# Graph and expert network on one core: the modulation moved one turn later on VectorE, and rows loaded four tiles ahead in the last row stage

## The chip, the core and the metric

The kernel is one program for one core of a Trainium2 chip. Its time is the device time of one execution in microseconds (us). Of the kernel before there are three runs: 3177.03 us in the median, 3170.88 the lowest, 3182.74 the highest. One more execution was recorded by the profiler, and all rows below are from it. The engines named here are PE (TensorE, matrix products and transposes), DVE (VectorE), ACT (ScalarE), POOL (GpSimd) and SP (SyncE, which here only issues transfers).

## What is computed

The reference adds four layers to `x` (1250 rows of 512 numbers): a graph layer over 20000 edges, a spline layer that sends each row to one of 64 experts, a graph transformer of four blocks, and a feed-forward layer with ternary weights. The change touches only the graph transformer's work on rows:

```python
def _cond_layer_norm(x, cond, sw, sb, bw, bb):
    mu = jnp.mean(x, axis=-1, keepdims=True)
    var = jnp.var(x, axis=-1, keepdims=True)
    xn = (x - mu) * jax.lax.rsqrt(var + EPS)
    return xn * (1.0 + (cond @ sw + sb)) + (cond @ bw + bb)

for i in range(4):
    y = _cond_layer_norm(x, cond, s1_w[i], s1_b[i], b1_w[i], b1_b[i])
    x = x + _sparse_attention(y, src, dst, wq[i], bq[i], wk[i], bk[i], wv[i], bv[i], wo[i], bo[i])
    y = _cond_layer_norm(x, cond, s2_w[i], s2_b[i], b2_w[i], b2_b[i])
    x = x + (jax.nn.relu(y @ m_w1[i] + m_b1[i]) @ m_w2[i] + m_b2[i])
```

The transformer's input is itself the normalised `x`, and `x` is added to its result at the end.

## The kernel before, in words

The 1250 rows are ten tiles of 125. Rows that don't fit on the chip's buffers lie in two tensors in device memory: `g_d` holds the transformer's running rows, `x_d` the rows of the layer around it. Between the attentions, which this change leaves alone, stands one function, `rows_stage`. It runs nine times:

- **the first stage** ("first" to "qkv"), once: the rows lie in a buffer already; norm, modulation, then the projections to queries, keys and values.
- **the attn-to-mlp stages**, four times: output projection of the attention added to the rows, norm, modulation, first half of the MLP.
- **the mlp-to-qkv stages**, three times: second half of the MLP added to the rows, norm, modulation, projections for the next block.
- **the last stage** ("mlp" to "final"), once: second half of the MLP, the rows of `g_d` and those of `x_d` summed and stored in `x_d`. It has no norm.

In a stage each engine has a written list of turns, one for each tile t from 0 to 9. Semaphores alone order the engines against each other; each engine does its own list strictly in order. With norm, the work on a tile goes through these steps (names of the code):

- SP `load(t)`: the tile's rows from `g_d` into one of four slots `g_row`. POOL adds a bias row (L1598).
- PE `src(t)`: the product that is added to the rows (L1470); not in the first stage.
- DVE `add(t)`: adds the product (L1806), then `bn_stats` and `bn_aggr` (L1808, L1810). SP then stores the rows to `g_d` (L1568).
- ACT `deviation(t)`, DVE `scales(t)` (L1814, L1816), ACT `center(t)` (L1708): the normalised row, in one of four slots `y_row`.
- PE `cond(t)`: 1+scale and bias of the condition, two products into two banks (L1632). There is one pair of banks, so `cond(t)` waits until `modulate(t-1)` has read it.
- DVE `modulate(t)`: y times scale plus bias, two instructions (L1823, L1825).
- PE `turn(t)`: four transposes of the row tile (L690). ACT `high(t)` copies them rounded (L1713), DVE `low(t)` takes the rest (L1829).
- PE `unit(n)`: twelve products of the turned rows with a weight matrix (L1461), from turn 7 on one for each turn, and after the turns all that are left. In the mlp stages ACT `take(n)` and DVE `finish(n)` (L1837) split each result.

In turns 3 to 6 DVE also splits a slice of the weights (`split`, L1797 or L1799).

The slots `g_row` are four. SP's list in the stages with norm, after the first four loads, is for each tile: wait for `added`, store tile t, then `load(t + 4)`, which first waits until that very store has landed, since the slot is the same. SP stands still in that wait, and the store of tile t+1 is behind it. In the last stage the list before is: store tile t, then `load(t + 2)`, whose slot was stored two turns earlier, and a load of the tile's `x_d` rows into one of two slots.

Of the kernel before, what the change touches and what calls it, by code (L numbers as in the profile page):

```python
# [18 lines left out]
ALU = mybir.AluOpType  # L19
# [3 lines left out]
P = 125  # L23
NT = N // P
# [1490 lines left out]
def rows_stage(nc, T, M, source, sink, g_d, x_d, loads, late, bias, bqk, bvo):  # L1515
# [5 lines left out]
    NCH = len(PARTS)  # L1521
    three = sink == "qkv"
    names = ("cw_in cw_ready cw_next b_in a_in w_in v_in a_high a_cut b_high b_cut v_high v_cut k_high k_cut "
             "g_in0 g_in1 g_in2 g_in3 gst0 gst1 gst2 gst3 x_in0 x_in1 o_high o_cut biased made added "
             "step std_s scale_s centered scaled row turned copied lowered "
             "unit_made taken h_high h_cut v_made v_row v_top v_low spare")
    with Stage(nc, names) as (cw_in, cw_ready, cw_next, b_in, a_in, w_in, v_in, a_high, a_cut, b_high, b_cut, v_high, v_cut,
                              k_high, k_cut, g_in0, g_in1, g_in2, g_in3, gst0, gst1, gst2, gst3, x_in0, x_in1,
                              o_high, o_cut, biased, made, added, step, std_s, scale_s, centered, scaled, row, turned,
                              copied, lowered, unit_made, taken, h_high, h_cut, v_made, v_row, v_top, v_low, spare):  # L1530
        g_in, gst, x_in = (g_in0, g_in1, g_in2, g_in3), (gst0, gst1, gst2, gst3), (x_in0, x_in1)
        cols = lambda t: slice(t * P, (t + 1) * P)
        turn_bank = lambda t: T.ps[:, 4 + t % 2, 0:4 * P].rearrange("p (c n) -> p c n", c=4)
        norm = sink != "final"
# [1 line left out]
        g = (lambda t: M.g[:, t % 4, :]) if pe_source else (lambda t: M.first[:, t, :])  # L1536
# [7 lines left out]
        with nc.Block() as block:  # L1544
            @block.sync
            def _(sp):
                def load(t):
                    if t >= 4:
                        if norm:
                            sp.wait_ge(centered, t - 3)  # L1550
                        sp.wait_ge(gst[t % 4], 16 * (t // 4))
                    sp.dma_start(g(t), g_d[t * P:(t + 1) * P, :]).then_inc(g_in[t % 4], 16)
                    if sink == "final":
                        if t >= 2:
                            sp.wait_ge(biased, t - 1)
                        sp.dma_start(M.y[:, t % 2, :], x_d[t * P:(t + 1) * P, :]).then_inc(x_in[t % 2], 16)
                ahead = 2 if sink == "final" else 4
                if pe_source:
                    load(0)
                    load(1)  # L1560
                if norm:
                    loads(sp, cw_in, b_in, w_in)
                if pe_source:
                    for t in range(2, ahead):
                        load(t)
                    for t in range(NT):
                        sp.wait_ge(added, t + 1)
                        sp.dma_start((g_d if norm else x_d)[t * P:(t + 1) * P, :], g(t)).then_inc(gst[t % 4], 16)  # L1568
                        if t + ahead < NT:
                            load(t + ahead)  # L1570
                if norm:
                    late(sp, cw_ready, cw_next, made, a_in, unit_made, v_in)
                if pe_source:
                    for t in range(NT - 4, NT):
                        sp.wait_ge(gst[t % 4], 16 * (t // 4 + 1))
                else:
                    sp.wait_ge(T.spilled, 64)

            @block.gpsimd
            def _(pool):  # L1580
                def o_lo(t):
                    pool.wait_ge(o_high, t + 1)
                    if t >= 3:
                        pool.wait_ge(made, t - 2)
                    nc.gpsimd.tensor_tensor(M.o[1][:, t % 3, :, :], M.q[:, :, cols(t)], M.o[0][:, t % 3, :, :].bitcast(F32),
                                            ALU.subtract).then_inc(o_cut, 1)
                if pe_source:
                    if source == "attn":
                        o_lo(0)
                    for t in range(NT):  # L1590
                        if source == "attn" and t + 1 < NT:
                            o_lo(t + 1)
                        pool.wait_ge(g_in[t % 4], 16 * (t // 4 + 1))
                        if sink == "final":
                            pool.wait_ge(x_in[t % 2], 16 * (t // 2 + 1))
                            nc.gpsimd.tensor_tensor(g(t), g(t), M.y[:, t % 2, :], ALU.add).then_inc(spare, 1)
                            pool.wait_ge(spare, t + 1)
                        nc.gpsimd.tensor_tensor(g(t), g(t), bias, ALU.add).then_inc(biased, 1)  # L1598

# [183 lines left out]
            def _(dve):  # L1783
# [9 lines left out]
                def split(raw, parts, hi_sem, sem, scale=1.0, ks=range(KD)):  # L1793
                    for k in ks:
                        dve.wait_ge(hi_sem, k + 1)
                        if scale == 1.0:
                            v.tensor_tensor(parts[1][:, k, :], raw[:, k, :], parts[0][:, k, :].bitcast(F32), ALU.subtract).then_inc(sem, 1)  # L1797
                        else:
                            v.scalar_tensor_tensor(parts[1][:, k, :], raw[:, k, :], scale, parts[0][:, k, :].bitcast(F32),  # L1799
                                                   ALU.mult, ALU.subtract).then_inc(sem, 1)  # L1800

                def add(t):
                    if pe_source:
                        dve.wait_ge(biased, t + 1)
                        dve.wait_ge(made, t + 1)
                        v.tensor_tensor(g(t), T.ps[0:P, t % 2, :], g(t), ALU.add).then_inc(added, 1)  # L1806
                        dve.wait_ge(added, t + 1)
                    v.bn_stats(T.stats[:, t, :], g(t)).then_inc(step, 1)  # L1808
                    dve.wait_ge(step, 2 * t + 1)
                    v.bn_aggr(T.mv[:, t, :], T.stats[:, t, :]).then_inc(step, 1)  # L1810

                def scales(t):
                    dve.wait_ge(std_s, t + 1)
                    v.reciprocal(T.rstd[:, t:t + 1], T.std[:, t:t + 1]).then_inc(scale_s, 1)  # L1814
                    dve.wait_ge(scale_s, 2 * t + 1)
                    v.scalar_tensor_tensor(T.shift[:, t:t + 1], T.mv[:, t, 0:1], -1.0, T.rstd[:, t:t + 1],  # L1816
                                           ALU.mult, ALU.mult).then_inc(scale_s, 1)

                def modulate(t):
                    y = M.y[:, t % 4, :]  # L1820
                    dve.wait_ge(scaled, t + 1)
                    dve.wait_ge(centered, t + 1)
                    v.scalar_tensor_tensor(y, T.ps[0:P, 2, :], 1.0, y, ALU.add, ALU.mult).then_inc(spare, 1)  # L1823
                    dve.wait_ge(spare, t + 1)
                    v.tensor_tensor(y, y, T.ps[0:P, 3, :], ALU.add).then_inc(row, 1)  # L1825

                def low(t):
                    dve.wait_ge(copied, t + 1)
                    v.tensor_tensor(M.yp[1][:, :, cols(t)], turn_bank(t), M.yp[0][:, :, cols(t)].bitcast(F32),  # L1829
                                    ALU.subtract).then_inc(lowered, 1)  # L1830
# [13 lines left out]
                if source == "attn":  # L1844
# [2 lines left out]
                v.tensor_tensor(M.cwr[32:64, :, :], T.cw[32:64, :, :], M.cwr[32:64, :, :].bitcast(F32),  # L1847
                                ALU.subtract).then_inc(cw_ready, 1)
                for t in range(NT):
                    add(t)  # L1850
                    if t >= 1:
                        scales(t - 1)
                    if t >= 2:
                        modulate(t - 2)
                    if t >= 8:
                        finish(t - 8)
                    if t >= 3:
                        low(t - 3)
                    if 3 <= t < KD + 3:
                        split(M.raw_b, M.b, b_high, b_cut, -DH ** -0.5 if three else 1.0, [t - 3])  # L1860
                scales(NT - 1)
                modulate(NT - 2)
                finish(2)
                low(NT - 3)
                modulate(NT - 1)
                finish(3)
                low(NT - 2)
                finish(4)
                finish(5)
                low(NT - 1)  # L1870
# [234 lines left out]
def second_graph_net(nc, T, A, x_scope, pairs, mask_d, x_d, g_d):  # L2105

    with ExitStack() as ctx:
# [49 lines left out]
        def attend(L, last):  # L2157
# [4 lines left out]
            rows_stage(nc, T, M, "attn", "mlp", g_d, x_d, *mlp_loads(L, last), bvo[:, 1, :], bqk, bvo)  # L2162

        rows_stage(nc, T, M, "first", "qkv", g_d, x_d, *qkv_loads(0, True), None, bqk, bvo)
        with nc.Fori(0, 3) as L:
            attend(L, False)
# [354 lines left out]
```

## Time and profile before

| | us |
|---|---|
| median of 3 runs | 3177.03 (3170.88 to 3182.74) |
| profiled execution, its own time | 3176.09 |
| its span, first to last instruction | 3174.4 |
| PE busy in the span | 2592.4 (82%) |
| DVE busy | 1889.8 (60%) |
| ACT busy | 1357.3 (43%) |
| POOL busy | 1127.8 (36%) |
| hardware queue of the transfers, share of 16 engines | 21.1% |

The nine row stages lie between 1077 and 2872 us of the span, with the four attentions between them. Busy shares of the whole span are means over stages with different limits, so what follows is read stage by stage from rows in order of time. A row of such a view has the start in us, the duration in us, the engine, the line, the operation, what it writes and reads, the count, and in brackets how long the engine had been idle before it and which instruction ended that wait.

### The profile page before, as it was taken

How to read it: one execution, taken by the hardware profiler on the slowest of the kernel's cores; microseconds unless marked ns; L12 is line 12 of the kernel's file. 1: busy time of each engine (PE TensorE's matmuls, PEld its weight loads, DVE VectorE, ACT ScalarE, POOL GpSimd, SP SyncE). 2: the span in 40 equal slices, each digit the busy share in tenths (PEclk: the TensorE clock that was granted, in tenths of full speed). 3: DMA queues.
4: the chain of work that ended last, by engine and by line, in shares of the span. 5: the costliest groups of instructions: out<-in, count | busy, mean ns of one | idle time of the engine just before them, and what ended most of it. 6: DMA issues, size and time to landing. Idle time of an engine off the chain costs nothing. (4 is left out here: it accounts for less than half of the span.)

```text
span 3174.4 us, 39503 instructions
## 1 busy us (share of the span) xinstructions
PE 2592.4 (82%) x13585; PEld 2210.9 (70%) x13585; DVE 1889.8 (60%) x3557; ACT 1357.3 (43%) x2706; POOL 1127.8 (36%) x886
## 2 busy tenths in 40 slices
PE   3999998347564299988889978989888899864999
PEld 3777877247364287876778966878767788653997
DVE  2899997523823536765456765367654567615862
ACT  2566664301343235653346643356543466412431
POOL 2777775856833002231012231022310122322420
PEclk9999999668677599999999999999999999886999
DMA  7344442157287302012211032120122110223101
GB/s 244 81 85 77 85 79 56 8 151 214 31 246 228 111 17 80 17 47 87 75 50 32 17 95 73 40 81 17 43 89 77 49 33 17 95 82 88 51 21 33
DMA packets 183070, 246.11 MB, mean 78 GB/s; under 512 B 110269, under 2 KB 118904, under 8 KB 175443
## 3 DMA queue, kind: packets, MB, share of 16 engines
q1 hardware_dynamic: 91312, 196.19, 21.1%
q0 software_dynamic: 91552, 47.27, 7.3%
q8 instruction: 118, 1.93, 0.3%
q14 instruction: 88, 0.72, 0.1%
HBM read 189.90 MB, written 52.95 MB: 77 GB/s over the span
## 5 line engine op out<-in xcount | busy, mean ns | idle before, releaser
L2101 POOL TENSOR_SCALAR prob<-prob,rden,linked 125x1250 f32<-125x1250 f32 x160 | 223.6, 1397 | 938.2 <-DVE rden L2068 938.2
L579 POOL DMA_INDIRECT pairs<-late_cnt,late_idx x160 | 345.2, 2157 | 124.2 <-issue 68.5
L2019 ACT CAST prob_high<-ps 125x375 fp32r<-125x375 f32 (+1 forms) x480 | 230.9, 503 | 266.8 <-PE ps L1981 266.5
L2060 DVE CUSTOM_DVE_ANT_0 prob<-ps,mask 125x1250 f32<-125x1250 f32 x160 | 233.1, 1457 | 124.9 <-PE ps L1957 111.5
L2073 DVE TENSOR_TENSOR prob_low<-ps,prob_high 125x375 fp32r<-125x375 f32 (+1 forms) x480 | 269.6, 585 | 46.6 <-ACT prob_high L2019 46.6
L338 POOL DMA_INDIRECT Hg<-h_rows,dsti x160 | 226.1, 1413 | 132.1 <-issue 93.7
L1970 PE MATMUL ps<-ident,prob 125*125 125x125 f32 x1600 | 252.4, 273 | 17.3 <-POOL prob L2101 10.6
L538 PE MATMUL ps<-onehot,mhi 125*128 125x512 f32 (+1 forms) x960 | 246.3, 365 | 9.7 <-DVE onehot L426 9.2
L1970 PEld LDWEIGHTS ps<-ident,prob 125*125 125x125 f32 x1600 | 232.4, 187 | 29.8 <-POOL prob L2101 22.9
L538 PE MATMUL ps<-onehot,mlo 125*128 125x512 f32 (+1 forms) x960 | 239.4, 358 | 0.0
L2011 ACT ACTIVATE prob<-prob,top 125x1250 f32<-125x1250 f32 x160 | 214.7, 1342 | 41.1 <-DVE top L2060 32.1
L1598 POOL TENSOR_TENSOR g_row<-g_row,bvo 125x512 f32<-125x512 f32 x80 | 103.7, 1296 | 351.9 <-DMA g_row<-g_d 350.8
L1981 PE MATMUL ps<-prob_high,v_high 125*128 125x376 f32 (+1 forms) x480 | 211.0, 440 | 4.6 <-ACT qT L2023 3.0
L1632 PE MATMUL ps<-cwr,condT 81*125 81x512 f32 x160 | 62.0, 472 | 180.3 <-DVE y_row L1825 98.2
L1957 PE MATMUL ps<-k_high,q_high 128*125 128x512 f32 (+1 forms) x480 | 174.2, 363 | 29.5 <-DVE q_low L2049 25.2
L538 PEld LDWEIGHTS ps<-onehot,mhi 125*128 125x128 f32 x960 | 158.8, 191 | 47.1 <-issue 18.4
L538 PEld LDWEIGHTS ps<-onehot,mlo 125*128 125x128 f32 x960 | 157.8, 191 | 28.3
L1957 PE MATMUL ps<-k_low,q_high 128*125 128x512 f32 (+1 forms) x480 | 172.5, 359 | 0.0
L1957 PE MATMUL ps<-k_high,q_low 128*125 128x512 f32 (+1 forms) x480 | 171.9, 358 | 0.0
L1632 PEld LDWEIGHTS ps<-cwr,condT 81*125 81x125 f32 x160 | 28.2, 205 | 205.1 <-DVE y_row L1825 120.2
L1981 PE MATMUL ps<-prob_high,v_low 125*128 125x376 f32 (+1 forms) x480 | 169.0, 352 | 0.0
L1981 PE MATMUL ps<-prob_low,v_high 125*128 125x376 f32 (+1 forms) x480 | 169.0, 352 | 0.0
(409 smaller groups left out, 6140.3 us busy)
## 6 DMA issues: line engine op xcount, KB each, us to landing
mask<-mask_d SPq DMA_DIRECT2D x40, 546.9 KB
g_row<-g_d SPq DMA_DIRECT2D x80, 250.0 KB
g_d<-g_row SPq DMA_DIRECT2D x70, 250.0 KB
sg_wd<-L_ffn_Wd SPq DMA_DIRECT2D x32, 512.0 KB
w_ring<-L_ffn_Wd SPq DMA_DIRECT2D x16, 1024.0 KB
w_ring<-L_ffn_Wu SPq DMA_DIRECT2D x16, 1024.0 KB
pairs<-zeros POOLq DMA_DIRECT2D x18, 625.0 KB, 26.2
keyrow<-keys_d SPq DMA_DIRECT2D x40, 244.1 KB
```

The lines of the kernel that those rows point to most:

```text
L338: nc.gpsimd.indirect_dma_start(Hg[:, g % 2, j, :, :].rearrange("p c f -> p (c f)"), None, h_rows[:, :], bass.IndirectOffsetOnAxis(dsti[:, ...
L538: ins = nc.tensor.matmul(agg_chunk(T, a, c), part[:, u, j, a * 128:(a + 1) * 128], onehot[:, j, n0:n0 + nn], start=first and k == 0 and c < 2,
L579: nc.gpsimd.indirect_dma_start(pairs[a][:, :], bass.IndirectOffsetOnAxis(T.E.late_idx[:, c:c + 1], 0), T.E.late_cnt[:, c:c + 1], None, com ...
L1598: nc.gpsimd.tensor_tensor(g(t), g(t), bias, ALU.add).then_inc(biased, 1)
L1957: ins = nc.tensor.matmul(S(u)[0:P, n0:n0 + nn], M.qr[x][:, b % 2, i * P:(i + 1) * P], M.k[y][:, h, n0:n0 + nn], start=n == 0, stop=n == 2)
L1970: ins = nc.tensor.transpose(T.ps[0:P, 3 + s % 4, i * P:(i + 1) * P], M.prob[:, (FIRST[b] + i) % RING, j * P:(j + 1) * P], T.ident[0:P, 0:P])
L1981: ins = nc.tensor.matmul(T.ps[:, 7, 0:w], M.v[x][:, j, h * DH:(h + 1) * DH], M.pt[y][:, s % 3, 0:w], start=j == 0 and n == 0, stop=j == NT ...
L2011: s.activation(M.prob[:, u % RING, :], M.prob[:, u % RING, :], ACT.Exp, bias=M.top[:, u % RING:u % RING + 1], scale=-1.0, accum_out=M.den[ ...
L2019: s.copy(M.pt[0][:, n % 3, 0:w], T.ps[0:P, 3 + n % 4, 0:w]).then_inc(high, 1)
L2060: v.tensor_tensor_reduce(M.prob[:, r, :], S(u)[0:P, 0:N], M.mask[:, it % MASKS, :], 1.0, 3.0e38, ALU.add, ALU.min, M.top[:, r:r + 1]).then ...
L2073: v.tensor_tensor(M.pt[1][:, n % 3, 0:w], T.ps[0:P, 3 + n % 4, 0:w], M.pt[0][:, n % 3, 0:w].bitcast(F32), ALU.subtract).then_inc(low, 1)
L2101: nc.gpsimd.tensor_scalar(M.prob[:, r, :], M.prob[:, r, :], M.rden[:, r:r + 1], T.linked[:, it:it + 1], ALU.mult, ALU.mult).then_inc(norme ...
```

## The change

It has two parts. In the stages with norm DVE's `modulate` of a tile moves: turn t no longer has `modulate(t-2)` after `scales(t-1)`, but begins with `modulate(t-3)`, ahead of `add(t)`; the calls behind the loop move with it. In the last stage `x_d` rows get four slots and four semaphores instead of two, and both loads run four tiles ahead. The lists of PE, ACT and POOL are the same.

```diff
                     if sink == "final":
-                        if t >= 2:
-                            sp.wait_ge(biased, t - 1)
-                        sp.dma_start(M.y[:, t % 2, :], x_d[t * P:(t + 1) * P, :]).then_inc(x_in[t % 2], 16)
-                ahead = 2 if sink == "final" else 4
+                        if t >= 4:
+                            sp.wait_ge(biased, t - 3)
+                        sp.dma_start(M.y[:, t % 4, :], x_d[t * P:(t + 1) * P, :]).then_inc(x_in[t % 4], 16)
...
-                    for t in range(2, ahead):
+                    for t in range(2, 4):
                         load(t)
...
-                        if t + ahead < NT:
-                            load(t + ahead)
+                        if t + 4 < NT:
+                            load(t + 4)
...
                 for t in range(NT):
+                    if t >= 3:
+                        modulate(t - 3)
                     add(t)
                     if t >= 1:
                         scales(t - 1)
-                    if t >= 2:
-                        modulate(t - 2)
                     if t >= 8:
                         finish(t - 8)
                     if t >= 3:
                         low(t - 3)
                     if 3 <= t < KD + 3:
                         split(M.raw_b, M.b, b_high, b_cut, -DH ** -0.5 if three else 1.0, [t - 3])
+                modulate(NT - 3)
                 scales(NT - 1)
-                modulate(NT - 2)
                 finish(2)
                 low(NT - 3)
-                modulate(NT - 1)
+                modulate(NT - 2)
                 finish(3)
                 low(NT - 2)
+                modulate(NT - 1)
```

DVE in the first stage, one turn (3 to 6), before: the modulation stands between `shift` and `y_low`.

```order
 L1808 BN_STATS stats<-first_rows 125x6
 L1810 BN_AGGR mv<-stats 125x2
 L1814 RECIPROCAL rstd<-std 125x1
 L1816 SCALAR_TENSOR_TENSOR shift<-mv,rstd 125x1
 L1823 SCALAR_TENSOR_TENSOR y_row<-ps,y_row 125x512
 L1825 TENSOR_TENSOR y_row<-y_row,ps 125x512
 L1829 TENSOR_TENSOR y_low<-ps,y_high 128x4x125
 L1799 SCALAR_TENSOR_TENSOR set_b_low<-set_b_raw,set_b_high 128x512
```

The same turn now (the new file's lines are one lower):

```order
 L1822 SCALAR_TENSOR_TENSOR y_row<-ps,y_row 125x512
 L1824 TENSOR_TENSOR y_row<-y_row,ps 125x512
 L1807 BN_STATS stats<-first_rows 125x6
 L1809 BN_AGGR mv<-stats 125x2
 L1813 RECIPROCAL rstd<-std 125x1
 L1815 SCALAR_TENSOR_TENSOR shift<-mv,rstd 125x1
 L1828 TENSOR_TENSOR y_low<-ps,y_high 128x4x125
 L1798 SCALAR_TENSOR_TENSOR set_b_low<-set_b_raw,set_b_high 128x512
```

Before, the `y_low` of turn t was of the tile that had been modulated in turn t-1; now it is of the tile whose modulation opens the same turn.

DVE in an attn-to-mlp stage, turn 9 and what stands behind it, before:

```order
 L1806 TENSOR_TENSOR g_row<-ps,g_row 125x512
 L1808 BN_STATS stats<-g_row 125x6
 L1810 BN_AGGR mv<-stats 125x2
 L1814 RECIPROCAL rstd<-std 125x1
 L1816 SCALAR_TENSOR_TENSOR shift<-mv,rstd 125x1
 L1823 SCALAR_TENSOR_TENSOR y_row<-ps,y_row 125x512
 L1825 TENSOR_TENSOR y_row<-y_row,ps 125x512
 L1837 TENSOR_TENSOR inner_low<-inner_row,inner_high 128x500
 L1829 TENSOR_TENSOR y_low<-ps,y_high 128x4x125
```

And now, from the same `add`:

```order
 L1805 TENSOR_TENSOR g_row<-ps,g_row 125x512
 L1807 BN_STATS stats<-g_row 125x6
 L1809 BN_AGGR mv<-stats 125x2
 L1813 RECIPROCAL rstd<-std 125x1
 L1815 SCALAR_TENSOR_TENSOR shift<-mv,rstd 125x1
 L1836 TENSOR_TENSOR inner_low<-inner_row,inner_high 128x500
 L1828 TENSOR_TENSOR y_low<-ps,y_high 128x4x125
 L1822 SCALAR_TENSOR_TENSOR y_row<-ps,y_row 125x512
 L1824 TENSOR_TENSOR y_row<-y_row,ps 125x512
```

The modulation of tile 7 now stands behind `finish` and `low`. In the mlp-to-qkv stages `finish` has no instruction there, and it stands behind `low` alone.

SP in the last stage, its first rows before:

```order
 L1552 DMA g_row<-g_d 125x512
 L1556 DMA y_row<-x_d 125x512
 L1552 DMA g_row<-g_d 125x512
 L1556 DMA y_row<-x_d 125x512
 L1568 DMA x_d<-g_row 125x512
 L1552 DMA g_row<-g_d 125x512
 L1556 DMA y_row<-x_d 125x512
```

And now:

```order
 L1556 DMA y_row<-x_d 125x512
 L1552 DMA g_row<-g_d 125x512
 L1556 DMA y_row<-x_d 125x512
 L1552 DMA g_row<-g_d 125x512
 L1556 DMA y_row<-x_d 125x512
 L1567 DMA x_d<-g_row 125x512
 L1552 DMA g_row<-g_d 125x512
 L1556 DMA y_row<-x_d 125x512
```

Four pairs of loads stand ahead of the first store instead of two, and the pair behind a store is of the tile four further on.

## Rows read from the trace of the kernel before

**Rows 1.** First stage by window: busy us of PE, PEld, DVE, ACT, POOL; clock.

```profile
1079.00:1103.00 24.00, 14.91 (x43) 10.48 (x44) 22.57 (x56) 11.83 (x24) 0.00 (x0) 0.52 0.03 12
```

**Rows 2.** First stage in order of time: first modulation, then a turn from the third.

```profile
1082.44 0.69 DVE L1823 SCALAR_TENSOR_TENSOR y_row<-ps,y_row 125x512 f32<-125x512 f32 x1
...
1088.87 0.69 DVE L1823 SCALAR_TENSOR_TENSOR y_row<-ps,y_row 125x512 f32<-125x512 f32 x1
...
1089.59 0.69 DVE L1825 TENSOR_TENSOR y_row<-y_row,ps 125x512 f32<-125x512 f32 x1
...
1090.20 0.67 DVE L1829 TENSOR_TENSOR y_low<-ps,y_high 128x500 fp32r<-128x500 f32 x1
...
1090.34 1.22 PE L1632 MATMUL ps<-cwr,condT 81*125 81x512 f32 x2 [1.65 <-DVE y_row L1825]
1090.79 0.68 DVE L1799 SCALAR_TENSOR_TENSOR set_b_low<-set_b_raw,set_b_high 128x512 fp32r<-128x512 f32 x1
...
1091.35 1.04 PE L690 MATMUL ps<-ident,y_row 125*128 125x125 f32 x4
...
1092.42 0.58 ACT L1713 CAST y_high<-ps 128x500 fp32r<-128x500 f32 x1 [1.71 <-PE ps L690]
```

**Rows 3.** First stage in order of time, PE when the units begin.

```profile
1097.50 1.22 PE L1632 MATMUL ps<-cwr,condT 81*125 81x512 f32 x2 [1.53 <-DVE y_row L1825]
...
1103.30 0.63 PE L1632 MATMUL ps<-cwr,condT 81*125 81x512 f32 x2
...
1106.92 0.63 PE L1632 MATMUL ps<-cwr,condT 81*125 81x512 f32 x2
```

**Rows 4.** Second attn-to-mlp stage in order of time, behind the last tile's add.

```profile
1892.56 0.69 DVE L1806 TENSOR_TENSOR g_row<-ps,g_row 125x512 f32<-125x512 f32 x1 [3.04 <-POOL g_row L1598]
...
1895.08 0.69 DVE L1825 TENSOR_TENSOR y_row<-y_row,ps 125x512 f32<-125x512 f32 x1
1895.68 0.67 DVE L1837 TENSOR_TENSOR inner_low<-inner_row,inner_high 128x500 fp32r<-128x500 f32 x1
...
1895.83 0.73 PE L1632 MATMUL ps<-cwr,condT 81*125 81x512 f32 x2 [3.54 <-DVE y_row L1825]
...
1896.28 0.67 DVE L1829 TENSOR_TENSOR y_low<-ps,y_high 128x500 fp32r<-128x500 f32 x1
...
1901.11 0.63 PE L1632 MATMUL ps<-cwr,condT 81*125 81x512 f32 x2
```

**Rows 5.** First mlp-to-qkv stage in order of time, behind the last tile's add.

```profile
1546.50 1.22 PE L1632 MATMUL ps<-cwr,condT 81*125 81x512 f32 x2 [3.38 <-DVE y_row L1825]
```

**Rows 6.** First attn-to-mlp stage, SP's own issues in order of time.

```profile
1415.94 0.25 SPq L1552 DMA_DIRECT2D g_row<-g_d  x1
1416.23 0.34 SPq L1568 DMA_DIRECT2D g_d<-g_row  x1
1423.10 0.25 SPq L1552 DMA_DIRECT2D g_row<-g_d  x1
```

**Rows 7.** Same stage, SP's waits: total us, times, longest us.

```profile
SPq L1551 <- DMA g_d<-g_row: 41.5, 6, 7.8
```

**Rows 8.** Last stage from 2806 to 2866 us, bytes moved in 40 slices.

```profile
GB/s 36 45 63 126 124 130 128 126 128 117 67 71 117 126 130 128 126 128 109 75 46 105 127 128 127 128 128 127 105 45 93 126 128 128 126 128 130 108 104 38
```

**Rows 9.** Last stage in order of time: SP's issues, and POOL's first sums.

```profile
2796.38 0.27 SPq L1552 DMA_DIRECT2D g_row<-g_d  x1
...
2802.91 1.26 POOL L1596 TENSOR_TENSOR g_row<-g_row,y_row 125x512 f32<-125x512 f32 x1 [37.10 <-DMA y_row<-x_d]
...
2806.27 0.25 SPq L1568 DMA_DIRECT2D x_d<-g_row  x1
...
2860.66 6.26 SPq L1568 DMA_DIRECT2D x_d<-g_row  x2
...
2863.32 1.26 POOL L1596 TENSOR_TENSOR g_row<-g_row,y_row 125x512 f32<-125x512 f32 x1 [3.41 <-DMA y_row<-x_d]
...
2871.86 0.36 SPq L2220 DMA_DIRECT2D raw<-L_ffn_w_gate  x1
```

More of the change, by code:

```diff
@@ L1523, in rows_stage @@
     names = ("cw_in cw_ready cw_next b_in a_in w_in v_in a_high a_cut b_high b_cut v_high v_cut k_high k_cut "
-             "g_in0 g_in1 g_in2 g_in3 gst0 gst1 gst2 gst3 x_in0 x_in1 o_high o_cut biased made added "
+             "g_in0 g_in1 g_in2 g_in3 gst0 gst1 gst2 gst3 x_in0 x_in1 x_in2 x_in3 o_high o_cut biased made added "
              "step std_s scale_s centered scaled row turned copied lowered "
@@ L1527, in rows_stage @@
     with Stage(nc, names) as (cw_in, cw_ready, cw_next, b_in, a_in, w_in, v_in, a_high, a_cut, b_high, b_cut, v_high, v_cut,
-                              k_high, k_cut, g_in0, g_in1, g_in2, g_in3, gst0, gst1, gst2, gst3, x_in0, x_in1,
+                              k_high, k_cut, g_in0, g_in1, g_in2, g_in3, gst0, gst1, gst2, gst3, x_in0, x_in1, x_in2, x_in3,
                               o_high, o_cut, biased, made, added, step, std_s, scale_s, centered, scaled, row, turned,
                               copied, lowered, unit_made, taken, h_high, h_cut, v_made, v_row, v_top, v_low, spare):
-        g_in, gst, x_in = (g_in0, g_in1, g_in2, g_in3), (gst0, gst1, gst2, gst3), (x_in0, x_in1)
+        g_in, gst, x_in = (g_in0, g_in1, g_in2, g_in3), (gst0, gst1, gst2, gst3), (x_in0, x_in1, x_in2, x_in3)
         cols = lambda t: slice(t * P, (t + 1) * P)
@@ L1594, in _ @@
                         if sink == "final":
-                            pool.wait_ge(x_in[t % 2], 16 * (t // 2 + 1))
-                            nc.gpsimd.tensor_tensor(g(t), g(t), M.y[:, t % 2, :], ALU.add).then_inc(spare, 1)
+                            pool.wait_ge(x_in[t % 4], 16 * (t // 4 + 1))
+                            nc.gpsimd.tensor_tensor(g(t), g(t), M.y[:, t % 4, :], ALU.add).then_inc(spare, 1)
                             pool.wait_ge(spare, t + 1)
```

## The prediction

> **What bounds the kernel now.** I read the views in this order: the page's slices for where the row stages lie, then each kind of row stage in order of time, then SP's own issues and waits, because there the engines are idle together. I looked for the instruction that the next one waits for, at the places where the change cuts a list.
>
> The first stage is bound by DVE until the units begin: it is busy 22.57 of 24.00 us, while PE has 14.91 us of work at a granted clock of 0.52, which is mostly the lower level of 1.2 GHz [rows 1]. A turn there is a chain over three engines as well. DVE's two modulation instructions start at 1088.87 and 1089.59 and end at 1090.28; PE's `cond` starts at 1090.34, the transposes at 1091.35, and they end at 1092.39; ACT's copy runs from 1092.42 to 1093.00 [rows 2]. Before, nothing in the same turn needs that copy. From the first unit on PE is the bound: `cond` to `cond` is 1106.92 - 1103.30 = 3.62 us [rows 3].
>
> The seven other stages with norm are paced by SP. In the cycle load, store, wait for the store, next load, SP needs 1423.10 - 1415.94 = 7.16 us [rows 6], and it stands in that wait 41.5 us in six times, at most 7.8 each [rows 7]. DVE and PE idle in them, until the last tile's `add`. Behind that PE is the bound again: it has idled 3.54 us when `modulate(7)` lets `cond(8)` go at 1895.83 [rows 4], 3.38 us in the other kind of stage [rows 5]; from there it has units without a pause to the stage's end.
>
> The last stage is bound by transfers. In the full slices they move 126 to 130 GB/s and never more [rows 8]. One tile's 125 x 512 f32 are 256,000 bytes, so a transfer takes 2.0 us at 128 GB/s and a tile's three take 6.0. The thin slices (36 to 75 GB/s) are where the next three have not been issued soon enough.
>
> **Part 1, DVE's order, first stage.** Nothing is added or removed; two instructions move by one place. Now `low(t-3)` needs, in its own turn, what the opening modulation starts. From the start of `modulate`: 1.47 us to `cond`, 1.01 to the transposes, 1.04 for them, 0.03, 0.58 for the copy, 0.03: `low` can start 4.16 us after it. Then 0.59 to `split` (1090.79 - 1090.20) and as much to the next modulation: 5.34 us for a turn [rows 2]. The statistics and `scales`, some 1.1 us, are hidden in that. The first modulation starts at 1082.44 in either order, since nothing is between `scales(1)` and it. Before, the fifth starts at 1097.50 - 1.47 = 1096.03, 13.59 us later [rows 2, 3]. Now it is 4 x 5.34 = 21.36 us later. The difference, 7.8 us, is how much later `cond(5)`, and so the first unit, runs. From unit 0 the same loop runs at the high clock: 1.47, 0.46 + 0.59 for the products (half of 1.01 and the transposes alike), 0.6 for the copy, 0.59 for `low` is about 3.7 against PE's 3.62, so 0.1 for each of three turns. I take +8.1 us; bounds are 1.1 (only the two calls that now stand ahead of `modulate(4)`, `low` and `split`, if the loop doesn't bind) and 10.
>
> **Part 1, the seven stages paced by SP.** In turns 4 to 9 DVE now does the moved modulation at once after the former turn, in the 3 us for which it waits for POOL [rows 4], so `add` starts when it did, and SP's cycle is untouched. PE runs its `cond` later and has idle time for it. What is late is the last turn: `cond(8)` waits for `modulate(7)`, and ahead of this now stand `finish(1)` and `low(6)` in the attn-to-mlp stages, 0.60 us each (1895.68 to 1896.28, and as long for `low`) [rows 4], and `low(6)` alone in the mlp-to-qkv stages. PE has no other work there. 4 x 1.2 + 3 x 0.6 = +6.6 us. The next one, `modulate(8)` behind `low(7)`, ends about 5.2 us after `cond(8)` starts and `cond(9)` is due 5.28 us after it [rows 4], so it just fits. If it doesn't, each stage loses up to 1 us more; if PE's later start is made up elsewhere, nothing is lost. Bounds 0 and 14.
>
> **Part 2, the last stage.** Two more pairs of loads go out at the start. Then for each tile SP issues store t, waits until it has landed, and only then loads tile t+4. Before, the slot had been stored two turns earlier and that wait was over. The trace shows the new cycle in the other stages, with one load: 7.16 us, of which 4.0 are two transfers and 3.2 the time until the store counts as landed [rows 6]. With two loads I take 6.0 + 3.2 = 9.2 us, against (2863.32 - 2802.91) / 9 = 6.7 for a tile before [rows 9]. For a load the tail is 2802.91 - 2796.38 - 4.0 = 2.5 us [rows 9].
> - Store 0 is the ninth transfer from 2796.38 (eight loads are ahead of it; it is issued at 2806.27) [rows 9]: landed at 2796.4 + 18.0 + 3.2 = 2817.6.
> - Load of tile 4 at 2817.6, of tile 9 five cycles later, at 2863.6; its `x_d` rows landed at 2863.6 + 4.0 + 2.5 = 2870.1.
> - From there to the next stage's first issue it is 2871.86 - 2863.32 = 8.5 us now [rows 9]. To it come 0.8 us, since stores 6, 7 and 8 are then queued behind the last loads, where before it was one: 2879.4 against 2871.86, +7.5 us.
>
> Tiles 2 and 3 get their rows sooner, and the last ones later. The bounds: -11.7 us, if SP never waits and 30 transfers run at 2.0 us from 2796.4 to 2856.4, plus 3.2 and the 0.6 to the next stage; +15, with the longest wait in every cycle (7.8 of wait and 0.6 of issues with one load [rows 7], 10.4 with two).
>
> The Trainium skill has a rule against my tail: "DMA: Bandwidth & Descriptors", section "Anatomy of one DMA", gives a DMA a fixed cost of about 2.0 us, most of it the receipt of the write, plus bytes by 436 GB/s. The row differs in both: 3.2 us behind the last byte, and 2.0 us for 256,000 bytes where the page's rate gives 0.6. By its 2.0 us alone the last stage would end as before, and the sum would be 3192 (an estimate from that page); by the rows it is 3199.
>
> **Sum.** 8.1 + 6.6 + 7.5 = 22.2 us. Against the profiled execution's own 3176.1 us (span 3174.4) that is 3198.3; that execution lies 0.9 under the median of the three runs, so I predict **3199 us**.
>
> **Rivals.**
> - *B, SP's wait costs nothing and the queue stays full.* Place: the last stage; -11.7 us there, decided if the loads of tiles 4 to 9 go out before the queue runs dry. Then 14.7 - 11.7 leaves 3180: not slower. For it: 12 us of the stage are thin slices [rows 8]. Against: SP stands in just this wait in seven stages [rows 7].
> - *C, a store lands as soon as a load does.* A tail of 2.5 instead of 3.2 in six cycles takes 4.2 us off: 3195. For it: only one shape of cycle is shown. The skill's rule named above stands here, with 3192.
> - *D, PE's pauses cost clock as well.* `cond(8)` to `cond(9)` is 5.28 us where it could be 3.62 at the high level [rows 3, 4]; all of it at 1.2 GHz would be 7.2. Then seven stages lose 2 us more: 3213. Against: PE's idle time before `cond(8)` stays as long as it was, since `cond(7)` is later too.
> - *E, faster.* B in the last stage, and the moved modulation finds PE's products done and gives back the waits inside the turns: nothing lost in the norm stages and a few us won, 3160. For it: DVE has `cond` one turn longer to wait for. Against: DVE is busy 94% of the first stage [rows 1] and waits for POOL in the others [rows 4].
>
> **How the numbers follow.** Forecast 0.62, B 0.12, C 0.14, D 0.08, E 0.04. The forecast's own range is 3190 to 3209: its three terms by their nearer bounds, and 3 us of spread between runs. With B partly left out and C and D taken in, the range is 3184 to 3209. What a measurement can tell from no change is 0.5%, 3161.1 to 3192.9. Slower than that: all but a tenth of the forecast, D, and part of C, less what I allow for errors common to all: 0.66. Within: B, the rest of C and of the forecast: 0.30. Faster: 0.04.
>
> **What would show it.** In the first stage modulations 5.3 us apart instead of 3.6, DVE idle before `y_low` with ACT's copy as releaser, and the first unit near 1107. In the attn-to-mlp stages `add` 7 to 8 us apart as now, and `cond(8)` 4.5 us behind the start of the last `add` instead of 3.27 (1895.83 - 1892.56) [rows 4]; in the mlp-to-qkv stages 3.9. In the last stage four pairs of loads, then SP issues 9.2 us apart, released by the store to `x_d`. I am wrong if those issues are under 7 us apart, if the units of the first stage start within 2 us of now, or if `add` in the seven stages moves.

## The result and the profile after

The changed kernel takes 3193.66 us in the median of its runs (3189.76 to 3203.71), the kernel before 3175.15 us beside it. The ratio is 1.0067, 95% interval 1.0056 to 1.0078, which is 21 us (it leaves out one disturbed run of the kernel before, which the median holds); the medians themselves lie 18.5 us apart. The forecast was 3199 us, with 0.66 on slower.

| profiled execution | before | after |
|---|---|---|
| own time, us | 3176.09 | 3193.53 |
| span | 3174.4 | 3191.8 |
| span before the first row stage | 1077.2 | 1072.8 |
| last row stage, first issue to the next stage's | 75.5 | 81.4 |

The two spans differ by 17.4 us, but the part ahead of the first row stage, which the change leaves alone, ran 4.4 us shorter in the execution after. So everything from the first row stage on took 21.8 us more, near what the ratio says. Lines of the new file are one lower than those of before.

**First stage.** One row by window, which answers to [rows 1] (busy us of PE, of PEld, which is PE's loading of weights, and of DVE, ACT and POOL; then the granted clock, the busy share of the 16 DMA engines, and GB/s):

```profile
1078.00:1102.00 24.00, 9.27 (x27) 6.21 (x28) 16.65 (x39) 8.94 (x18) 0.00 (x0) 0.50 0.02 8
```

DVE has 16.65 us of work in 24 where it had 22.57. The same stretch in order of time (start, duration, engine, line, operation; in brackets the idle time before and what ended it), for [rows 2]:

```profile
1088.76 0.68 DVE L1822 SCALAR_TENSOR_TENSOR y_row<-ps,y_row 125x512 f32<-125x512 f32 x1
1089.48 0.69 DVE L1824 TENSOR_TENSOR y_row<-y_row,ps 125x512 f32<-125x512 f32 x1
...
1090.22 1.22 PE L1631 MATMUL ps<-cwr,condT 81*125 81x512 f32 x2 [3.30 <-DVE y_row L1824]
...
1091.24 1.03 PE L690 MATMUL ps<-ident,y_row 125*128 125x125 f32 x4
1092.31 0.58 ACT L1712 CAST y_high<-ps 128x500 fp32r<-128x500 f32 x1 [3.36 <-PE ps L690]
...
1092.92 0.68 DVE L1828 TENSOR_TENSOR y_low<-ps,y_high 128x500 fp32r<-128x500 f32 x1 [1.69 <-ACT y_high L1712]
...
1093.52 0.68 DVE L1798 SCALAR_TENSOR_TENSOR set_b_low<-set_b_raw,set_b_high 128x512 fp32r<-128x512 f32 x1
...
1094.12 0.68 DVE L1822 SCALAR_TENSOR_TENSOR y_row<-ps,y_row 125x512 f32<-125x512 f32 x1
```

The loop can be walked with a finger: modulation, `cond`, transposes, ACT's copy, `y_low`, `split`, and the next modulation 5.36 us after the last. `y_low` waits 1.69 us, released by ACT's copy, and PE's wait before `cond` has grown to 3.30 us. PE when the units begin, for [rows 3]:

```profile
1100.93 1.21 PE L1631 MATMUL ps<-cwr,condT 81*125 81x512 f32 x2 [3.30 <-DVE y_row L1824]
...
1106.87 0.64 PE L1631 MATMUL ps<-cwr,condT 81*125 81x512 f32 x2
...
1110.63 0.73 PE L1631 MATMUL ps<-cwr,condT 81*125 81x512 f32 x2
...
1118.68 0.73 PE L1631 MATMUL ps<-cwr,condT 81*125 81x512 f32 x2 [0.28 <-DVE y_row L1824]
```

`cond(5)`, the first of these rows, stands 22.88 us behind the first modulation (1078.05), where it stood 15.06 behind (1097.50 - 1082.44): +7.8 us. From `cond(6)` at 1106.87 to `cond(9)` at 1118.68 it takes 11.81 us, where it took 10.89 before, and the last row shows PE waiting there for the late modulation. From the first modulation to the attention's first product the stage takes 118.82 us against 109.84, +9.0.

**Seven stages paced by SP.** The second attn-to-mlp stage behind its last `add`, for [rows 4], and under it the row of the first mlp-to-qkv stage, for [rows 5]:

```profile
1898.80 0.69 DVE L1805 TENSOR_TENSOR g_row<-ps,g_row 125x512 f32<-125x512 f32 x1 [3.28 <-POOL g_row L1597]
...
1900.60 0.67 DVE L1836 TENSOR_TENSOR inner_low<-inner_row,inner_high 128x500 fp32r<-128x500 f32 x1
1901.18 0.67 DVE L1828 TENSOR_TENSOR y_low<-ps,y_high 128x500 fp32r<-128x500 f32 x1
1901.77 0.68 DVE L1822 SCALAR_TENSOR_TENSOR y_row<-ps,y_row 125x512 f32<-125x512 f32 x1
1902.49 0.69 DVE L1824 TENSOR_TENSOR y_row<-y_row,ps 125x512 f32<-125x512 f32 x1
...
1903.23 0.72 PE L1631 MATMUL ps<-cwr,condT 81*125 81x512 f32 x2 [3.76 <-DVE y_row L1824]
...
1908.51 0.63 PE L1631 MATMUL ps<-cwr,condT 81*125 81x512 f32 x2
```

```profile
1552.37 0.78 PE L1631 MATMUL ps<-cwr,condT 81*125 81x512 f32 x2 [3.17 <-DVE y_row L1824]
```

`finish` and `low` now stand ahead of `modulate(7)`, and `cond(8)` starts 1903.23 - 1898.80 = 4.43 us behind the last `add` instead of 3.27; in the other kind of stage it is 1552.37 - 1548.54 = 3.83 us instead of 3.27. `cond(9)` follows 5.28 us later, as before. SP's issues (marked SPq) and its wait in the first attn-to-mlp stage, for [rows 6, 7]:

```profile
1420.93 0.25 SPq L1552 DMA_DIRECT2D g_row<-g_d  x1
1421.22 0.34 SPq L1567 DMA_DIRECT2D g_d<-g_row  x1
1428.32 0.25 SPq L1552 DMA_DIRECT2D g_row<-g_d  x1
```

```profile
SPq L1551 <- DMA g_d<-g_row: 41.0, 6, 7.8
```

Nothing moved there: 41.0 us of wait against 41.5.

**Last stage.** Bytes moved in 40 slices of 1.5 us from 2817 us on (for [rows 8]), then SP's waits in it (total us, times, longest):

```profile
GB/s 127 127 126 126 124 124 108 12 57 127 96 113 107 11 76 120 79 111 113 8 56 128 105 111 105 10 66 127 109 126 75 14 85 126 108 126 55 26 109 116
```

```profile
SPq L1552 <- DMA x_d<-g_row: 49.3, 6, 10.3
```

Once in every six slices the transfers fall to 8 to 26 GB/s. In most of such a slice nothing is queued: SP waits for the store that it has just sent. In order of time, for [rows 9]:

```profile
2807.45 0.27 SPq L1552 DMA_DIRECT2D g_row<-g_d  x1
...
2813.34 1.80 SPq L1556 DMA_DIRECT2D y_row<-x_d  x1
...
2813.85 1.26 POOL L1595 TENSOR_TENSOR g_row<-g_row,y_row 125x512 f32<-125x512 f32 x1 [37.12 <-DMA y_row<-x_d]
...
2817.20 0.38 SPq L1567 DMA_DIRECT2D x_d<-g_row  x1
...
2827.89 0.25 SPq L1552 DMA_DIRECT2D g_row<-g_d  x1
2828.18 0.34 SPq L1556 DMA_DIRECT2D y_row<-x_d  x1
2828.57 0.34 SPq L1567 DMA_DIRECT2D x_d<-g_row  x1
2836.80 0.25 SPq L1552 DMA_DIRECT2D g_row<-g_d  x1
...
2872.10 0.25 SPq L1552 DMA_DIRECT2D g_row<-g_d  x1
...
2879.25 1.26 POOL L1595 TENSOR_TENSOR g_row<-g_row,y_row 125x512 f32<-125x512 f32 x1 [6.45 <-DMA y_row<-x_d]
...
2888.80 0.36 SPq L2220 DMA_DIRECT2D raw<-L_ffn_w_gate  x1
```

The first store is in and the next load goes out 20.4 us after the stage's first issue; then five cycles of (2872.10 - 2827.89) / 5 = 8.84 us.

### The profile page after: what moved, and what is told of

It is laid out like the page before. It is cut to its first block and busy times, and to the rows that moved or that the text cites. A ratio compares the mean times of both kernels' runs of the same rounds, so it can differ in the third digit from the quotient of the medians.

```text
span 3191.8 us, 39507 instructions
## 1 busy us (share of the span) xinstructions
PE 2594.4 (81%) x13585; PEld 2213.3 (69%) x13585; DVE 1885.8 (59%) x3557; ACT 1357.8 (43%) x2706; POOL 1144.3 (36%) x886
## 5 line engine op out<-in xcount | busy, mean ns | idle before, releaser
L579 POOL DMA_INDIRECT pairs<-late_cnt,late_idx x160 | 353.9, 2212 | 120.7 <-issue 69.4
```

Source lines behind the costliest of these rows:

```text
L579: nc.gpsimd.indirect_dma_start(pairs[a][:, :], bass.IndirectOffsetOnAxis(T.E.late_idx[:, c:c + 1], 0), T.E.late_cnt[:, c:c + 1], None, com ...
```

## The experiments

Ratios are to the kernel before on the same chip, with 95% intervals. Each theory's words stand as they were written ahead of the run.

**Each part alone.** `late_mod` puts the change's moves on DVE under a condition. The first of the two lines is that of the run with the first stage alone, the second that of the run with the seven; the other moves are put under `late_mod` in the same way.

```diff
+                late_mod = source == "first"
...
+                late_mod = source != "first"
...
+                    if late_mod and t >= 3:
+                        modulate(t - 3)
```

> Only the first stage has the new order on VectorE, everything else is as before. My account (the modulation opens a loop modulate, cond, transposes, ACT's copy, low, split of 5.34 us that DVE can't leave): cond(5) 22.9 us behind the first modulation instead of 15.1, and the whole kernel +7.8 us, 0.25%. Rival, that the order only shifts two calls and the loop doesn't bind: +1 us. Rival, that the difference lies outside the row stages (code loading, another start): under 2 us and no change of that distance.

Measured: 3184.39 against 3173.02 us, ratio 1.003 (1.0017 to 1.0043). From the first modulation, 1079.02, to `cond(5)`, 1101.90, it is the same 22.88 us as in the whole change, and to the attention's first product 118.48 us.

> Only the seven later stages with norm have the new order on VectorE, the first and the last are as before. My account: add times as before, cond(8) 4.43 us behind the last add in the four attn-to-mlp stages and 3.84 in the three mlp-to-qkv stages instead of 3.27; in sum 4 x 1.16 + 3 x 0.57 = +6.4 us, 0.2%. Rival, that DVE's later modulation holds the adds up: adds further apart than 7.3 us and more than +12. Rival, that PE makes it up: 0.

Measured: 3180.55 us, ratio 1.0026 (1.0012 to 1.0039). `cond(8)` stands 4.43 us behind the last `add` in all four attn-to-mlp stages and 3.84 in the three others: 4 x 1.16 + 3 x 0.58 = 6.4 us. The `add`s didn't move: first to last they take 370.6 us in the seven stages together, against 372.7 before.

> Only the last stage is changed: loads four tiles ahead, four slots for the x_d rows. My account (SP stands in the wait for the store that it has just issued): issues of g_row loads 8.8 us apart from tile 4 on, +6 us, 0.19%. Rival, that more transfers in flight run each slower: the full slices under 126 GB/s. Sum of this run and the two beside it should be the whole change, +20 us.

The edit is the change's part 2 alone. Measured: 3180.59 us, ratio 1.0019 (1.0006 to 1.0033). Issues to load tiles 4 to 9 go out from 2816.98 to 2862.01, 9.0 us apart, and the stage takes 82.8 us against 75.5, +7.4 where the whole change had +5.9. The three parts sum to +0.75%, the whole is +0.67%, each with some 0.12 of doubt: within that they add up.

**Is it the loop, in the first stage?** If `low` of a tile goes one turn later as well, the loop is open again while the modulation stays late.

```diff
-                    if t >= 3:
-                        low(t - 3)
+                    if t >= 3 + late_mod:
+                        low(t - 3 - late_mod)
```

> The first stage has the late modulation as in the run with the first stage alone, but low also stands one turn later (low(t-4) in turn t), so that no call of a turn needs what the opening modulation of the same turn starts. My account (the loop over three engines costs, not the modulation's place): modulations 3.58 us apart again, cond(5) 15.2 us behind the first modulation, the whole kernel 0 to +1 us against before. Rival, that beginning the turn with the modulation costs by itself (it delays statistics and scales, and with them center): still +5 us or more.

Measured: 3177.73 against 3177.55 us, ratio 1.0 (0.9991 to 1.001). The last modulation ahead of the units, and its `cond(5)`, in order of time:

```profile
1098.28 0.69 DVE L1823 SCALAR_TENSOR_TENSOR y_row<-ps,y_row 125x512 f32<-125x512 f32 x1
...
1099.74 1.22 PE L1632 MATMUL ps<-cwr,condT 81*125 81x512 f32 x2 [1.52 <-DVE y_row L1825]
```

It is 15.17 us behind the first modulation (1084.57), against 15.06 before, and the second to the fifth modulation stand 3.57 us apart. The late modulation by itself costs nothing, within 0.1%; what costs is that the same turn needs what ACT makes of its result.

**Is it only the two calls, in the seven stages?** Turns 3 to 8 have the late modulation. Turn 9 has both, `modulate(6)` at its head and `modulate(7)` at its old place, and the calls behind the loop are as before.

```diff
-                    if t >= 2:
+                    if (not late_mod and t >= 2) or (late_mod and t == NT - 1):
                         modulate(t - 2)
```

> The seven later stages with norm have the late modulation, but turn 9 also has modulate(7) directly behind scales(8), and the calls behind the loop are as before; first and last stage as before. My account (only the calls ahead of modulate(7) cost): cond(8) 3.27 us behind the last add in all seven, the whole kernel 0 against before. Rival, that the late modulation of turns 4 to 8 pushes PE back and the tail inherits it: cond(8) later than 3.27, still +3 us or more.

Measured: 3175.05 us, ratio 0.9994 (0.9985 to 1.0002). `cond(8)` in the second attn-to-mlp stage, whose last `add` starts at 1880.32:

```profile
1883.59 0.72 PE L1632 MATMUL ps<-cwr,condT 81*125 81x512 f32 x2 [2.36 <-DVE y_row L1825]
```

It is 3.27 us again, and the whole kernel's time is that of before. The late modulation in the turns is free there; only what stands ahead of `modulate(7)` is paid. In two of the seven stages `cond(9)` also follows 1.6 us sooner than before, 3.1 us in sum that the account doesn't name; the places of `cond(8)` are the firmer proof.

**The store that SP waits for.** With four slots, loads three tiles ahead need the slot of the tile before the one just stored.

```diff
-                ahead = 4 if sink == "final" else 4
+                ahead = 3 if sink == "final" else 4
```

> As the run with the last stage changed alone, but three tiles ahead instead of four. With three the slot was stored one turn earlier: when SP waits for that store, the transfers of one more tile are still queued behind it. My account: the queue never runs dry, issues 6.1 us apart, the last stage 9 us shorter than before and 15 shorter than with four: -9 us against before, 3167. Rival, that the depth itself costs (contention, more transfers in flight): between two and four ahead, so +3 us.

Measured: 3164.54 against 3173.02 us, ratio 0.9969 (0.9957 to 0.9981). Bytes moved in 40 slices of the last stage from 2796 us on, and SP's loads for two tiles:

```profile
GB/s 96 137 127 128 127 126 126 122 123 130 130 126 127 130 126 127 130 130 123 130 130 123 130 130 126 127 130 128 124 130 130 123 130 130 124 128 128 127 127 48
```

```profile
2810.91 0.25 SPq L1552 DMA_DIRECT2D g_row<-g_d  x1
...
2816.92 0.25 SPq L1552 DMA_DIRECT2D g_row<-g_d  x1
```

No thin slice is left, and a tile takes 6.0 us, three transfers of 2.0. The stage takes 65.2 us (2794.48 to 2859.70) against 75.5 before: -10.3 us, where rival B's price for a queue that stays full was -11.7. That one number, three instead of four, turns +0.19% into -0.31%: what the stage lost was lost in the empty queue.

**The 128 GB/s themselves.** The kernel has a helper, `wide` (L140), that sends a tile of 125 rows as two transfers, of 112 and of 13. Here it carries the last stage's transfers, the semaphores counting 32 for each tile; the loads are three tiles ahead.

```diff
+                def move(dst, src, sem):
+                    if WIDE:
+                        wide(sp, dst, src, sem)
...
-                    sp.dma_start(g(t), g_d[t * P:(t + 1) * P, :]).then_inc(g_in[t % 4], 16)
+                    move(g(t), g_d[t * P:(t + 1) * P, :], g_in[t % 4])
```

> Last stage alone, three tiles ahead, and each transfer of 125 rows issued as one of 112 rows and one of 13. My account (a transfer of 125 rows runs at 5 of the 16 engines' rate, 2.0 us, and that is what bounds the stage): full slices well over 130 GB/s, tiles 3 to 3.5 us apart, bound by POOL's two sums and PE, the stage 30 to 36 us shorter than before. Rival, that 128 GB/s is what rows of 2 KB get in any split: the same 6 us for a tile, and -9 us as with three ahead alone.

Measured: 3139.49 against 3177.55 us, ratio 0.9877 (0.986 to 0.9895). The same stretch of the stage, six tiles, by window in this kernel; the last two numbers are the busy share of the 16 DMA engines and GB/s:

```profile
2807.65:2825.10 17.45, 17.35 (x75) 13.23 (x74) 4.15 (x6) 0.00 (x0) 15.05 (x12) 1.00 0.85 252
```

and in the kernel with unsplit transfers and the same distance, five tiles:

```profile
2810.91:2840.96 30.05, 19.75 (x69) 13.95 (x67) 3.46 (x5) 0.00 (x0) 12.71 (x11) 0.89 0.33 128
```

Bytes flow at 252 instead of 128 GB/s, the DMA engines are busy 85% instead of 33% of the time, and the `add`s come 2.95 us apart ((2832.70 - 2806.14) / 9). PE is busy 17.35 of 17.45 us, at a granted clock of 1.00, the high level, and POOL 15.05: PE bounds the stage now. From its first issue to the next stage's it takes 38.15 us (2798.88 to 2837.03), 37.3 less than before, where 30 to 36 were expected.

> The order of before, the last stage three ahead, and every tile transfer of the eight stages in two pieces of 112 and 13 rows. My account: SP's cycle falls from 7.3 to about 5.2 us (3.2 of wait, 1.3 of transfers, the issues), and PE with 6.4 us for a turn takes over from turn 7 on: 8 to 11 us less in each of seven stages and 30 to 36 in the last, in sum -90 to -110 us, 3080. Rival, that the wait for the store hardly shrinks with the transfer: under 3 us in each of the seven.

The same for all transfers of tiles in the eight stages; DVE's order is as before, and the last stage's loads are three tiles ahead. Measured: 3035.26 against 3177.55 us, ratio 0.955 (0.9537 to 0.9564): 142 us less, the best of all kernels here. SP's wait in the first attn-to-mlp stage ([rows 7] before), and the last `add` with `cond(8)` and `cond(9)` there (lines are 8 higher):

```profile
SPq L1559 <- DMA g_d<-g_row: 11.9, 6, 2.3
```

```profile
1441.00 0.69 DVE L1814 TENSOR_TENSOR g_row<-ps,g_row 125x512 f32<-125x512 f32 x1 [2.05 <-PE ps L1470]
...
1444.36 0.63 PE L1640 MATMUL ps<-cwr,condT 81*125 81x512 f32 x2
...
1447.99 0.62 PE L1640 MATMUL ps<-cwr,condT 81*125 81x512 f32 x2
```

The wait for a store falls from 41.5 to 11.9 us, and what ends DVE's wait for `add` is now PE, not POOL. First to last `add` takes 40.7 us instead of 53.2 in this stage, and `cond(8)` to `cond(9)` 3.63 instead of 5.29. By window (the number behind the five engines is the granted clock), that stretch in the second attn-to-mlp stage before:

```profile
1895.83:1901.11 5.28, 5.28 (x18) 4.31 (x19) 3.91 (x8) 2.46 (x4) 0.00 (x0) 0.68 0.64 236
```

and the one above in this kernel:

```profile
1444.36:1447.99 3.63, 3.63 (x19) 3.03 (x19) 2.80 (x7) 2.27 (x4) 0.00 (x0) 1.00 0.80 247
```

PE had been idle 3.54 us before the first of these two windows [rows 4], and then works at a clock of 0.68, partly at 1.2 GHz; here, with no pause ahead of `cond(8)`, it works at 2.4 GHz. I had expected 90 to 110 us. Between the profiled spans there are 132: 86 by `add` spacing in seven stages (11.2 to 13.3 each, where 8 to 11 were expected), 13 by the stretch from the last `add` to `cond(9)` in them, which I had not counted, and 35 by the last stage (30.99 us from its first `add` to its end, before 66.31), against 2 the other way elsewhere.

**The change once transfers are fast.** Last, the whole change over the split transfers, and the split transfers with only the distance of four.

> The changed order in all stages with norm and the last stage four tiles ahead, with every tile transfer of the eight stages split 112+13. Against the kernel that has only the split transfers and three tiles ahead (its span 3042.4 us, ratio 0.955): first stage +7.8 us as before. In the seven others the calls ahead of modulate(7) still cost 4 x 1.2 + 3 x 0.6 = 6.6 us; and cond(9) is now due 3.63 us behind cond(8) where modulate(8) takes about 5.2, so up to 1.6 us more in each of seven, 11 us. Last stage: SP's wait for the store in each cycle, the difference that the kernel sent beside this one measures, about +10. Sum +35 us, span near 3078, ratio near 0.966. Rival: with SP no longer pacing (adds 5.5 us apart), DVE's order matters inside the turns, and having each cond one turn longer gives waits back: add spacing under 5.3 us, ratio 0.955 or less.

> Split transfers in all eight stages, the order of before, the last stage four tiles ahead instead of three: that one number is the difference from the kernel with ratio 0.955. Account of the dry queue: SP stands behind each store until it has landed; in the other stages with split transfers load to load is 3.9 us with one load, so with two about 5.2, against 3.0 a tile with three ahead. Six such cycles, less what the first loads gain: +10 us (8 to 14), ratio near 0.958. Rival: with fast transfers four pairs in flight cover the wait and nothing is lost: within 2 us of 0.955.

Measured against 3176.81 us: with the distance of four 3046.78 us, ratio 0.9598 (0.9575 to 0.9621); with the moved modulation as well 3068.8 us, ratio 0.9655 (0.9635 to 0.9675). The moved modulation costs 18 us here by the ratios, 22 by the medians, where 25 was expected. Of this the traces have 7.8 in the first stage up to `cond(5)`, 5.7 ahead of `cond(8)` in the seven (4 x 1.07 + 3 x 0.47), and a new wait: `cond(9)` comes 4.95 and 4.18 us behind `cond(8)` instead of 3.63, since `modulate(8)` is late, 4 x 1.32 + 3 x 0.55 = 6.9 us of the 11 allowed for. The first of the two products of `cond(9)` in the first attn-to-mlp stage, with the wait:

```profile
1451.78 0.50 PE L1640 MATMUL ps<-cwr,condT 81*125 81x512 f32 x1 [1.06 <-DVE y_row L1833]
```

In sum these are 20.4 us. The eight stages with norm are 25.3 longer in all; of the 4.9 us more, 3.8 are `add` spacing. First to last `add` takes 40.5 us in the attn-to-mlp stages, where it is 40.7 with the order of before (42.3 once), and 42.2 to 44.1 in the mlp-to-qkv stages, where it is 40.2 to 42.4. So the rival, waits given back inside the turns, finds at most 0.2 us in a stage and loses more elsewhere. The distance of four has load issues 2724.24 - 2700.53 = 23.7 us for five tiles, 4.74 each, where three ahead gives (2723.53 - 2706.00) / 6 = 2.92, and 38.78 us from the stage's first `add` to its end where it was 30.99: +7.8 us in the trace. By the ratios it is 0.48%, 15 us, with intervals 0.11% apart: a loss is shown, its size only roughly.

## Why the prediction was right

**First stage, +8.1 predicted.** The loop was worked out at 5.34 us from rows of before that never showed it closed, and it is 5.36; the later start of `cond(5)` was put at 7.8 and is 7.8. The run with `low` one turn later shows that the cause is this loop and not the order as such. The lesser claim, 0.1 for each of the three turns with units at the high clock, was too small: from `cond(6)` to `cond(9)` the steps are 3.77, 3.87 and 4.18 us in all three traces with the new order in this stage (within 0.02), and 3.62, 3.63 and 3.64 before, 0.9 more in sum instead of 0.3. The last step has `cond(9)` waiting for `modulate(8)`, which the sum had not counted here. So the term is 8.6 (the run with the first stage alone) to 9.0 us rather than 8.1.

**Seven stages, +6.6 predicted.** 6.4 by the traces of both the change and the run with this part alone: 0.58 us for each call instead of 0.60. The claims that hold it up held too: SP's wait is unchanged, `modulate(8)` just fits (it ends at 1908.12, `cond(9)` starts at 1908.51), and with the old order behind the last turn the loss is gone.

**Last stage, +7.5 predicted, 5.9 measured** (81.35 against 75.48 us). The mechanism was right and its size off by 1.6 in this trace; in that of the run with the last stage alone the stage has +7.4. The term that was off is the store's tail, the time from a store's last byte until SP goes on, 3.2 us, taken from a cycle with one load. With two loads the cycle is 8.84 us, a tail of 2.8, and behind the eight first loads it is 20.4 - 18.0 = 2.4. This brought the last load 2.5 us earlier than forecast (64.65 us behind the first issue, not 67.2). Against it, tile 9's rows took 7.15 us to land where I had 6.5, and the end behind them 9.55 where I had 9.3. Why a tail is 2.4, 2.8, 3.0 (9.0 - 6.0 in the run with the last stage alone) or 3.4 us (7.39 - 4.0 in the cycle with one load) the runs don't settle.

**Rivals.** *B* fell: the queue stays full only three ahead, and then it gives 10.3 of B's 11.7 us. *C* was half right: the tail of 2.8 lies midway between a load's 2.4 (2813.85 - 2807.45 - 4.0) and my 3.2. By the Trainium skill's fixed cost behind it ("DMA: Bandwidth & Descriptors", section "Anatomy of one DMA — SWDGE (gpsimd) path") the stage would not grow (the prediction's estimate); the trace has 5.9 us. That section gives its figure for transfers issued from GpSimd, and these are issued from SP, so the difference does not speak against the page; the prediction should have said so. *D* finds nothing in the change's trace: `cond(8)` to `cond(9)` is 5.3 us in five of the seven stages after and 6.5 and 6.6 in two, and before it is 5.3 in five, 6.2 and 6.5 in two. But the trace with the seven stages alone has five of them at 6.1 to 6.6, and the traces with the old order and unsplit transfers in these stages have one to three. With one trace of each kernel, a small share for D can't be told from this scatter. The clock is lost in either kernel. *E* fell with B; no kernel here won anything by the later modulation.

**The total.** 22.2 us were forecast; the loss is 21.3 us by the ratio, 18.5 between the medians and 21.8 between the profiles. That it comes so near is in part luck: the last stage's term was 1.6 too large in this trace and the first stage's 0.9 too small. Nor are the 21.8 us all in the row stages. These differ by 19.4 (9.0 in the first, 4.5 in the seven from first issue to end, 5.9 in the last), the four attentions between them by 2.0 and what follows by 0.5, though the change touches neither. In the seven the 6.4 us behind the last `add` stand against a scatter of each stage's length by 1 to 2 us between executions. Of the 5.3 us between 3199 and 3193.66, 1.9 are the base (a median of 3177.03 in the runs shown, 3175.15 in those beside the change), and the rest is that the medians differ by less than was forecast.

## What to carry to other kernels

- When a producer is moved later in an engine's turn, look whether the same turn's later instructions need what other engines make of it. If so the turn becomes that loop, and its length can be added up from rows that never show it closed.
- Where one engine is free in the turns, moving work costs only behind the last turn: count what now stands ahead of the instruction that the bound engine waits for.
- A load ahead by as many tiles as there are slots waits for the store just issued; one less keeps the queue full. The same wait read in another stage gave the cycle within some 4% (9.2 us for 8.84).
- A flat ceiling in the bytes moved (128 GB/s, the DMA engines a third busy) is itself something to ask about: splitting the transfers, with loads three ahead in the last stage, gave 142 us, where the change moved 21.

## What the hardware showed that was not expected

- Transfers of 125 rows of 2 KB keep the 16 DMA engines busy a third of the time though the queue has no gap: share 0.33, with slices at 122 to 137 GB/s. As 112 and 13 rows the same bytes go at 252 GB/s, share 0.85. The Trainium skill ("DMA: Bandwidth & Descriptors", section "Why a DMA increments its semaphore by 16 and not by 1") says that a DMA uses the largest number of engines up to 16 that divides its slowest dimension: 5 for 125 rows, 16 for 112. The traces agree: 5 of 16 is 0.31, and the trace with three tiles ahead and unsplit transfers has exactly five packets in flight at 83% of the instants from 2812 to 2839 us. Its packets under 512 bytes point the same way: 70 from 2811 to 2840 us, beside 1807 of 2 KB, are 4.8 for every 125 rows; with split transfers 484 beside 2088 (2808 to 2825 us) are 29.0, which is 16 + 13.
- SP itself is held up by a long queue: of the eight loads issued at the start of the last stage the issues of the first five take 0.27 to 0.67 us each and those of the last three 1.8, about one transfer's time.
- A pause of PE can cost time behind it as well: the same instructions from `cond(8)` to `cond(9)` take 5.28 us at a granted clock of 0.68 behind an idle 3.54 us, and 3.63 at 1.00 without it. The length of the pause alone doesn't decide it. With the late modulation and the old order behind the last turn they take 3.7 us in the first and second attn-to-mlp stages, behind 2.24 and 2.36 us of pause, but 5.3 in the third and fourth, behind 2.14 and 2.34.
